# The bias of the output projection: from a matmul in each tile to a GpSimd addition on each tile of x

## The chip, the cores and the metric

The program runs on one core of one Trainium2 chip, in one launch. The metric is the device time of that core in microseconds (us), the median of several runs; less is better. The engines are named as the profile names them: PE (TensorE, with PEld for its weight loads), DVE (VectorE), ACT (ScalarE), POOL (GpSimd) and SP, whose queue issues most of the transfers.

## The reference, cut to what matters

```python
# x: [8, 1024, 512] float32; 16 heads of 32
qkv = x @ W_attn + b_attn
scores = k.q / sqrt(32), causal mask; attn = softmax over the keys
out = (attn @ v) reshaped to [8, 1024, 512]
x = layernorm(x + (out @ W_out + b_out))            # b_out: [512]
# then, per batch: the 1024 rows with the highest router score go through
# gelu(x @ W1 + b1) @ W2 + b2, are weighted, added back, and layernorm again
```

The change concerns `out @ W_out + b_out + x`. In the kernel the bias that is added is `b_out` plus the value part of `b_attn` times `W_out`, a single row of 512 numbers.

## The kernel before

**Units.** Attention is worked off in 64 units: a unit `u` is one batch, one group of four heads and one half `c = u % 2` of the queries (512). A half with c = 0 has 4 steps of 128 keys, one with c = 1 has 8 (`ksteps`). A step (u, k) is written here as (c, k).

**Slots and beats.** The program is laid out on a clock of slots of 16 beats, by the class `Table`. All five engine programs loop over the same beats `n`, and each engine does in beat `n` what the table puts there, in order; the engines meet only at semaphores. Two slots, an even and an odd one, are a period: they hold the scores of one odd and one even unit, and so on. The names in the code:

- `a_piece` (L1404) makes scores whose row maxima DVE takes (L1042, L1050); three PSUM banks in a ring. The maxima are turned (L1411), copied by DVE (L1061, L1063) and sent to `Qp` as a shift.
- `b_tile` (L1438) makes the scores again, transposed and shifted, in two PSUM banks in turn; ACT takes their exponential (L943) into one of `Pa`, `Pm` (two) and `P3` (in the trace `P`). A step's tiles must be read by ACT before PE can write the bank anew.
- POOL adds each step's probabilities onto `Pa`, head by head (L818), for the softmax sums, and clears the upper triangle of the diagonal steps with `keep` (L795). `pv` (L1456) on PE multiplies by V, and waits for `keep` where the step is on the diagonal. The buffer of step a is written again by ACT three steps later, once POOL has added it and PE has used it.
- `dense` on PE makes one piece (mostly one matmul) at a time of the projections in between: jobs K, Q (L1352), V (L1360), O (L1366, L1368), N (the softmax sums, L1375), with two PSUM banks taken in turn by the order of the jobs. A job waits for the evacuation of the job two before it.

**The output projection.** There are 64 jobs O, one for each tile of 128 rows. The first is in slot 10; up to batch 6 there is one in each slot, in beats 11 to 14, and those of batch 7 end in the slots after the last unit, between the first steps of the feed-forward part. Job `o` has its x tile in `xb[:, o % 2]`, loaded by SP (L708) some nine beats before the job starts, or, in the last batch, as late as one beat after it, since the slot must be stored first (L703, `ost`). PE does twelve matmuls of the split product and a thirteenth, `ones[0:97, :]` by `CB[0:97, :]` (L1368), which adds the bias: row 0 of `CB` is its high part and row 96 its rest. DVE then adds the PSUM tile onto `xb` (L1120), takes its statistics (L1122, L1253); POOL makes the scale and shift from them (L827, L828, L831, L834), and ACT writes the normalised tile to `hs` (L998) and to `xb` (L1000), which SP stores (L701, L703).

In POOL's program the additions of the steps formed in a beat stand first, then the four small instructions of the O job that ended in the beat before:

```python
for n in range(T.first, T.last):
    for u, k in T.steps_formed(n):
        ...
    for j in o_beat.get(n - 1, ()):
        ...
        e.wait_ge(s["lmva"], o + 1)
```

After the attention part comes the feed-forward part, from about 1880 us on; some of its steps are laid between the last O jobs.

Of the kernel before, what the change touches and what calls it, by code (L numbers as in the profile page):

```python
# [5 lines left out]
F32 = mybir.dt.float32  # L6
F32R = mybir.dt.float32r
# [6 lines left out]
P = 128  # L14
# [111 lines left out]
def dense_jobs(slot):  # L126
# [20 lines left out]
    if slot == 1:  # L147
        jobs.append(("C",))
    if 0 <= slot - 2 < U:
        jobs.append(("N", slot - 2))  # L150
# [4 lines left out]
PIECES = {"K": [1] * 12, "Q": [1] * 12, "V": [1] * 12, "O": [1] * 13, "T": [2], "S": [1], "N": [4], "C": [4] * 4}  # L155
TICKS = 54
# [18 lines left out]
class Table:  # L175
# [103 lines left out]
    def vector_in(self, n):  # L279

        now = self.ended.get(n, [])
        return [j for j in self.ended.get(n - 1, []) if j[0] in "KQT"] + [
            j for j in self.ended.get(n - 2, []) if j[0] == "N"] + [j for j in now if j[0] in "OCS"]
# [79 lines left out]
def layer(nc, s, args, dr, cs, out):  # L363
    T = Table()
    x, xt, wqkv, wo, bat, b_out, w_router, W1, b1, W2, b2 = args
    with ExitStack() as st:
# [63 lines left out]
        CB = sb("CB", [P, D], F32R)  # L430
# [13 lines left out]
        crow = hs[0:1, 0, :]  # L444
        ones = sb("ones", [P, P], F32R)
# [115 lines left out]
        o_beat, o_conv, o_load, t_load = T.o_beat, T.o_conv, T.o_load, T.t_load  # L561
        o_store = {}
# [186 lines left out]
        def gpsimd(e):  # L749
# [48 lines left out]
            for n in range(T.first, T.last):  # L798
                for u, k in T.steps_formed(n):
# [4 lines left out]
                    if a is not None and not by_products(u) and not in_sums(u, k):  # L804
# [9 lines left out]
                        for h0 in range(0, HG, many):  # L814
                            if h0 == (0 if k + 2 == ksteps(u) else 2) and kept_early(u, k + 1):
# [3 lines left out]
                                            ALU.add).then_inc(s["padd"], many)  # L819
                for j in o_beat.get(n - 1, ()):  # L820
# [205 lines left out]
        def vector(e):  # L1026
# [52 lines left out]
            def evacuate(job):  # L1079
# [27 lines left out]
                elif job[0] == "C":  # L1107
# [6 lines left out]
                    e.tensor_tensor(CB[96:97, :], crow, CB[0:1, :].bitcast(F32), ALU.subtract).then_inc(s["ev_v"], 1)  # L1114
                else:
# [3 lines left out]
                    e.wait_ge(s["xb", o % 2], 16 * (o // 2 + 1))  # L1119
# [177 lines left out]
        def tensor(e):  # L1297
            def wait_ready(job):
# [18 lines left out]
                elif kind == "T":  # L1317
                    e.wait_ge(s["hg", 0], 64)
                elif kind == "S":
                    e.wait_ge(s["score"], TT * (job[1] + 1))  # L1320
                else:
                    e.wait_ge(s["os"], o_number(job) + 1)
                    if o_number(job) == 0:
                        e.wait_ge(s["wo_lo"], 2)
                        e.wait_ge(*freed(("C",)))
# [11 lines left out]
            def dense(job, k):  # L1337
# [24 lines left out]
                elif kind == "O":  # L1362
                    if k < 12:
                        term, kt = divmod(k, KT)
                        oh, wh = ((0, 0), (1, 0), (0, 1))[term]
                        ins = e.matmul(to, Os[:, oh, kt, :], Wo[wh][:, kt, :], start=k == 0, stop=False)  # L1366
                    else:
                        ins = e.matmul(to, ones[0:97, :], CB[0:97, :], start=False, stop=True)  # L1368
# [13 lines left out]
                elif kind == "S":  # L1382
                    ins = e.transpose(to[0:TT, 0:P], sc[:, job[1], :], cs["identf"][:])
                else:
# [174 lines left out]
        with nc.Block() as block:  # L1559
# [8 lines left out]
              "wo_hi", "wo_lo", "x_hi", "x_lo", "ones", "rows", "d_mm", "ev_v", "ev_a", "kq_hi", "a_mm", "a_max",  # L1568
# [63 lines left out]
```

## Time and profile before

| | |
|---|---|
| median of 3 runs | 2560.07 us (2559.65 to 2562.88) |
| span of the profiled execution | 2558.8 us |
| PE busy | 2481.7 us (97%), 14168 matmuls |
| DVE, ACT, POOL busy | 1665.5 (65%), 1190.7 (47%), 1556.9 us (61%) |
| chain that ended last | PE 81%, POOL 2%, ACT 2%, DVE 1%, DMA 1% |
| mean granted TensorE clock | 0.981 |
| L1368, the thirteenth matmul | x64, 395 ns each in the trace |
| POOL busy, feed-forward part (1880 to 2558 us) | 154.76 of 678 us; PE 666.12 |

The profiled execution's span is 1.3 us under the median of the runs; that difference is the little that lies around the span. A matmul's time in the trace is that from its start to its last result; the next one starts before that, so what one costs PE is the distance between starts.

### The profile page before, as it was taken

What the parts mean: (1) busy time and instruction counts of PE and PEld (TensorE: products, weight loads), DVE (VectorE), ACT (ScalarE), POOL (GpSimd) and SP (SyncE); (2) the same over time, 40 slices, a digit from 0 to 9 for tenths busy, and PEclk for the clock granted to TensorE, in tenths of its full rate; (3) what the DMA queues carried; (4) which work ended last, traced back from release to release, by engine and by line L of the source; (5) the groups of instructions that cost most, each with busy time, mean ns of one, the idle gap of its engine ahead of it and who ended that gap; (6) DMA issues with size and microseconds to landing.
All of it is one profiled execution on the core that took longest, in us unless ns stands there. A gap on an engine that the chain in (4) does not pass through costs nothing.

```text
span 2558.8 us, 40698 instructions
## 1 busy us (share of the span) xinstructions
PE 2481.7 (97%) x14168; PEld 1834.9 (72%) x14168; DVE 1665.5 (65%) x4231; ACT 1190.7 (47%) x2034; POOL 1556.9 (61%) x1635
## 2 busy tenths in 40 slices
PE   7999999999999999999999999997999999999998
PEld 5666676777776777777776767773688888888886
DVE  6667677777776867877677777777555545553533
ACT  2555566656655655656656556565531111111110
POOL 1677788778887878888778877877232113121211
PEclk8999999999999999999999999998999999999999
DMA  7666677776577866767766676763420101010000
GB/s 146 90 108 139 126 144 172 140 150 157 129 144 130 193 128 127 175 127 153 151 145 146 125 167 137 155 154 97 152 91 25 34 25 42 25 34 25 22 29 17
DMA packets 167262, 286.46 MB, mean 112 GB/s; under 512 B 23121, under 2 KB 58001, under 8 KB 165906
## 3 DMA queue, kind: packets, MB, share of 16 engines
q1 hardware_dynamic: 159890, 267.01, 49.1%
q0 software_dynamic: 7168, 16.85, 2.1%
q8 instruction: 114, 1.87, 0.4%
q14 instruction: 90, 0.74, 0.1%
HBM read 116.97 MB, written 65.11 MB: 71 GB/s over the span
## 4 chain that ended last, share of the span: by engine, by line
PE 81%; POOL 2%; ACT 2%; DVE 1%; issue 1%; DMA 1%; SPq 1%; POOLq 0%; ACTq 0%; DVEq 0%
PE PS L1512 13%; PE PS L1491 13%; PE PS L1352 11%; PE PS L1438 10%; PE PS L1404 9%; PE PS L1456 8%; PE PS L1366 7%; PE PS L1360 6%; PE PS L1375 2%; POOL Pa L818 1%; PE PS L1368 1%; PE PS L1472 0%; PE PS L1333 0%; DMA h_s<-hs 0%; ACT Pm L943 0%
## 5 line engine op out<-in xcount | busy, mean ns | idle before, releaser
L818 POOL TENSOR_TENSOR Pa<-Pa,Pm 128x512 f32<-128x512 f32 (+1 forms) x602 | 743.8, 1259 | 114.4 <-ACT Pm L943 101.5
L1438 PE MATMUL PS<-Qp,Kp 98*128 98x512 f32 (+3 forms) x1536 | 494.9, 358 | 24.1 <-ACT Pm L943 13.2
L1404 PE MATMUL PS<-Kp,Qp 96*128 96x512 f32 (+3 forms) x1536 | 495.0, 359 | 17.4 <-DVE nm L1042 5.7
L943 ACT ACTIVATE Pm<-PS 128x512 f32<-128x512 f32 (+1 forms) x643 | 358.1, 568 | 282.6 <-PE PS L1438 243.5
L1042 DVE TENSOR_REDUCE nm<-PS 128x1 f32<-128x512 f32 x512 | 344.9, 687 | 183.7 <-PE PS L1404 183.6
L818 POOL TENSOR_TENSOR Pa<-Pa,P 128x512 f32<-128x512 f32 (+1 forms) x297 | 369.6, 1268 | 57.1 <-ACT P L943 50.1
L1404 PEld LDWEIGHTS PS<-Kp,Qp 96*128 96x128 f32 x1536 | 282.9, 193 | 118.5 <-issue 44.3
L1438 PEld LDWEIGHTS PS<-Qp,Kp 98*128 98x128 f32 x1536 | 281.7, 192 | 104.1 <-ACT Pm L943 27.4
L1050 DVE CUSTOM_DVE_ANT_0 PS<-PS,maskA 128x384 f32<-128x384 f32 (+3 forms) x512 | 245.9, 509 | 153.3 <-PE PS L1404 152.2
L908 ACT ACTIVATE G<-PS,b1c 128x512 f32<-128x512 f32 x128 | 88.2, 689 | 539.6 <-PE PS L1491 539.5
L1050 DVE CUSTOM_DVE_ANT_0 PS<-PS,maskA,nm 128x384 f32<-128x384 f32 (+3 forms) x512 | 267.0, 554 | 91.6 <-PE PS L1404 85.9
L1512 PE MATMUL PS<-W2h,Gs 128*128 128x512 f32 x1024 | 316.7, 390 | 0.9 <-DVE W2l L1144 0.9
L1491 PE MATMUL PS<-hT,W1h 128*128 128x512 f32 x1024 | 271.9, 389 | 0.0
L1195 DVE CAST Gs<-G 128x512 fp32r<-128x512 f32 x128 | 54.6, 427 | 306.9 <-ACT G L908 246.5
L943 ACT ACTIVATE P<-PS 128x512 f32<-128x512 f32 (+1 forms) x317 | 176.5, 569 | 132.8 <-PE PS L1438 115.1
L1491 PEld LDWEIGHTS PS<-hT,W1h 128*128 128x128 f32 x1024 | 192.1, 188 | 40.3 <-issue 0.2
L1512 PEld LDWEIGHTS PS<-W2h,Gs 128*128 128x128 f32 x1024 | 191.1, 188 | 40.0 <-issue 1.3
L943 ACT ACTIVATE Pa<-PS 128x512 f32<-128x512 f32 x256 | 149.1, 598 | 124.8 <-PE PS L1438 124.6
L1512 PE MATMUL PS<-W2l,Gs 128*128 128x512 f32 x512 | 199.2, 389 | 0.0
L783 POOL TENSOR_SCALAR rs<-mv 128x1 f32<-128x1 f32 x32 | 9.6, 301 | 304.8 <-DVE mv L1179 302.9
L1352 PE MATMUL PS<-xTh,Wkh 128*128 128x512 f32 x512 | 183.9, 412 | 8.8 <-ACT xTh L919 6.9
L1352 PE MATMUL PS<-xTh,Wkl 128*128 128x512 f32 x512 | 182.8, 411 | 0.0
(142 smaller groups left out, 4236.4 us busy)
## 6 DMA issues: line engine op xcount, KB each, us to landing
Qp<-nat SPq DMA_DIRECT2D x192, 256.0 KB, 7.4
Kp<-nat SPq DMA_DIRECT2D x192, 256.0 KB, 6.2
o_s<-Of SPq DMA_DIRECT2D x64, 256.0 KB, 2.3
Ot<-o_s SPq DMA_DIRECT2D x64, 256.0 KB, 3.1
xb<-in_x SPq DMA_DIRECT2D x64, 256.0 KB, 3.2
h_s<-hs SPq DMA_DIRECT2D x64, 256.0 KB, 2.3
out<-xb SPq DMA_DIRECT2D x64, 256.0 KB, 2.5
x_raw<-in_xt SPq DMA_DIRECT2D x15, 1024.0 KB, 6.4
```

The lines of the kernel that those rows point to most:

```text
L818: e.tensor_tensor(to, to, probs(u, k)[:, h0:h0 + many, 0:w], ALU.add).then_inc(s["padd"], many)
L943: e.activation(probs(u, k)[:, hh[0]:hh[-1] + 1, 0:w], tile_bank(j)[:, 0:len(hh) * w].rearrange("p (h n) -> p h n", n=w), ACT.Exp).then_inc ...
L1042: ins = e.tensor_reduce(out=nm[:, u % 2, 0, hh[0], qt:qt + 1], in_=PS[:, A_BANKS[j % 3], :], op=ALU.max, axis=AX, negate=True)
L1050: ins = e.tensor_tensor_reduce(out=to, in0=to, in1=maskA[:, 512 - w:512], scale=-1.0, scalar=least, op0=ALU.add, op1=ALU.min, accum_out=nm ...
L1352: ins = e.matmul(to, Wk[wh][:, 1 if kind == "K" else 0, kt, :], xT[xh][:, kt, c * 512:c * 512 + 512], start=k == 0, stop=k == 11)
L1360: ins = e.matmul(to[:, t * 256:t * 256 + 256], xT[xh][:, kt, tok:tok + P], Wv[wh][:, kt, :], start=m == 0, stop=m == 11)
L1366: ins = e.matmul(to, Os[:, oh, kt, :], Wo[wh][:, kt, :], start=k == 0, stop=False)
L1404: ins = e.matmul(to, Qp[0:96, u % 4, h_, qt * P:qt * P + P], Kp[0:96, (2 * i + k0 // 512) % 4, h_, 0:w], start=True, stop=True)
L1438: ins = e.matmul(tile_bank(j)[:, x_ * w:x_ * w + w], Kp[0:98, (2 * i + k // 4) % 4, h_, k % 4 * P:k % 4 * P + P], Qp[0:98, u % 4, h_, 512 ...
L1456: ins = e.matmul(PO[32 * h_:32 * h_ + 32, 512 - w:512], V[:, (u // 4 * 4 + k // 2) % 6, k % 2, vo:vo + HD], probs(u, k)[:, h_, 0:w], start ...
L1491: ins = e.matmul(PS[:, UP_BANKS[j % 2], :], W1p[wh][k][:, f * P:f * P + P], hT[:, xh, k, :], start=n_ == 0, stop=n_ == 11)
L1512: ins = e.matmul(PS[:, DOWN_BANK + t, :], Gs[:, j % 3, gh, t * P:t * P + P], W2p[wh][f // 4][:, f % 4, :], start=f == 0 and n_ == 0, stop= ...
```

## The change

The bias row is spread over the 128 partitions once, by one matmul of `ones` by `CB` (a new job R in slot 2) which DVE copies into the new tile `cB`. Job O has twelve matmuls, and the table has 53 ticks in a slot and not 54; no O job starts or ends in another beat, but 30 of the 64 Q jobs and 31 of the 64 V jobs end one beat later. At the beat in which an O job starts on PE, POOL adds `cB` to its x tile, behind the additions of that beat and ahead of the small instructions of the job before. DVE's addition of the PSUM tile waits for POOL's (`xc`) and no longer for the load of x. `CB` now lies in the space of `Os`.

```diff
@@ dense_jobs
+    if slot == 2:
+        jobs.append(("R",))
@@
-PIECES = {..., "O": [1] * 13, ...}
-TICKS = 54
+PIECES = {..., "O": [1] * 12, ..., "R": [4]}
+TICKS = 53
@@ layer
-        CB = sb("CB", [P, D], F32R)
+        cB = sb("cB", [P, D], F32)
+        CB = Os[:, 0, :, :].rearrange("p k n -> p (k n)")
+        biased = {}
+        for j in T.o_jobs:
+            biased.setdefault(T.start[j], []).append(j)
@@ gpsimd, in beat n, behind the additions of the steps
+                for j in biased.get(n, ()):
+                    o = o_number(j)
+                    if o == 0:
+                        e.wait_ge(*freed(("R",)))
+                    e.wait_ge(s["xb", o % 2], 16 * (o // 2 + 1))
+                    y = xb[:, o % 2, :]
+                    e.tensor_tensor(y, y, cB[:, :], ALU.add).then_inc(s["xc"], 1)
                 for j in o_beat.get(n - 1, ()):
@@ vector, evacuate
+                elif job[0] == "R":
+                    e.wait_ge(*done(job))
+                    e.tensor_copy(cB[:, :], src).then_inc(s["ev_v"], 1)
                 else:
                     o = o_number(job)
                     y = xb[:, o % 2, :]
                     e.wait_ge(*done(job))
-                    e.wait_ge(s["xb", o % 2], 16 * (o // 2 + 1))
+                    e.wait_ge(s["xc"], o + 1)
                     e.tensor_tensor(y, src, y, ALU.add).then_inc(s["ev_v"], 1)
@@ tensor, dense
-                    if k < 12:
-                        ...
-                    else:
-                        ins = e.matmul(to, ones[0:97, :], CB[0:97, :], start=False, stop=True)
+                    ... start=k == 0, stop=k == 11)
+                elif kind == "R":
+                    ins = e.matmul(to, ones[0:97, :], CB[0:97, :], start=True, stop=True)
```

Three places of POOL's queue. The first is the even slot with the O job number 26 (counted from 0), where the additions of an odd unit begin; L818 of before is L825 of the changed kernel, L795 is L802, and L827, L834 are L841, L848. Before:

```order
L818 TENSOR_TENSOR Pa<-Pa,P 128x512 [waits s_pv,s_padd,s_b_exp]
L818 TENSOR_TENSOR Pa<-Pa,P 128x512 x3
L818 TENSOR_TENSOR Pa<-Pa,Pm 128x512 [waits s_padd,s_b_exp]
L818 TENSOR_TENSOR Pa<-Pa,Pm 128x512 x3
L827 TENSOR_SCALAR lnrs<-lnmv 128x1 [waits s_oset,s_lmva]
```

In the changed kernel, at the same place:

```order
L825 TENSOR_TENSOR Pa<-Pa,P 128x512 [waits s_pv,s_padd,s_b_exp]
L825 TENSOR_TENSOR Pa<-Pa,P 128x512 x3
L833 TENSOR_TENSOR xb<-xb,cB 128x512 [waits s_xb_0]
L825 TENSOR_TENSOR Pa<-Pa,Pm 128x512 [waits s_padd,s_b_exp]
L825 TENSOR_TENSOR Pa<-Pa,Pm 128x512 x3
L841 TENSOR_SCALAR lnrs<-lnmv 128x1 [waits s_oset,s_lmva]
```

The addition of the bias stands between the four additions of step (1, 1) and those of step (1, 2), and ahead of everything that follows for the odd unit. The second is the odd slot behind it (job 27). Before:

```order
L795 AFFINE_SELECT P<-P 128x4x128 [waits s_b_exp,s_padd,s_keep]
L818 TENSOR_TENSOR Pa<-Pa,Pm 128x2x256 x2
L795 AFFINE_SELECT Pa<-Pa 128x4x128 [waits s_b_exp]
L827 TENSOR_SCALAR lnrs<-lnmv 128x1 [waits s_oset,s_lmva]
```

And in the changed kernel:

```order
L802 AFFINE_SELECT P<-P 128x4x128 [waits s_b_exp,s_padd,s_keep]
L825 TENSOR_TENSOR Pa<-Pa,Pm 128x2x256 x2
L833 TENSOR_TENSOR xb<-xb,cB 128x512 [waits s_xb_1]
L802 AFFINE_SELECT Pa<-Pa 128x4x128 [waits s_b_exp]
L841 TENSOR_SCALAR lnrs<-lnmv 128x1 [waits s_oset,s_lmva]
```

Here it stands behind the last `keep` (step (1, 7)) and the last additions of the odd unit, and ahead of the first `keep` of the next one. The third place is the last batch, where POOL has nothing else left. In the changed kernel (before, the same without L833):

```order
L833 TENSOR_TENSOR xb<-xb,cB 128x512 [waits s_xb_0]
L841 TENSOR_SCALAR lnrs<-lnmv 128x1 [waits s_oset,s_lmva]
L842 TENSOR_SCALAR lnrs<-lnmv 128x1
L845 TENSOR_TENSOR lnrs<-lnrs,half 128x2 [waits s_p_link]
L848 TENSOR_SCALAR lnnb<-lnrs,lnmv 128x2 [waits s_p_link]
```

There the addition for job `o`, which waits for the load of x tile `o`, stands ahead of the small instructions of job `o - 1`.

## Rows read from the trace of the kernel before

**Rows 1.** Windows: length, then each engine's busy us (instructions), PEclk, DMA share, GB/s.

```profile
1010.10:1042.00 31.90, 31.90 (x183) 22.04 (x181) 23.69 (x57) 18.23 (x33) 31.01 (x30) 1.00 0.58 103
1042.00:1063.60 21.60, 21.56 (x160) 16.25 (x160) 16.21 (x47) 15.44 (x28) 11.80 (x15) 1.00 0.87 217
```

**Rows 2.** Timeline of PE at the thirteenth matmul: start, length, engine, line, shapes, count.

```profile
1014.39 0.40 PE L1438 MATMUL PS<-Qp,Kp 98*128 98x512 f32 x1
1014.62 0.40 PE L1368 MATMUL PS<-CB,ones 97*128 97x512 f32 x1
1014.85 0.40 PE L1404 MATMUL PS<-Kp,Qp 96*128 96x512 f32 x1
```

**Rows 3.** Timeline of POOL over the additions of one odd unit (u = 35).

```profile
1010.11 5.03 POOL L818 TENSOR_TENSOR Pa<-Pa,P 128x512 f32<-128x512 f32 x4 [5.24 <-ACT P L943]
1015.28 5.00 POOL L818 TENSOR_TENSOR Pa<-Pa,Pm 128x512 f32<-128x512 f32 x4
...
1021.71 0.27 POOL L834 TENSOR_SCALAR lnnb<-lnrs,lnmv 128x2 f32<-128x2 f32 x1
1021.93 5.01 POOL L818 TENSOR_TENSOR Pa<-Pa,Pm 128x512 f32<-128x512 f32 x4
...
1038.83 0.64 POOL L795 TENSOR_SCALAR_AFFINE_SELECT P<-P 128x512 f32<-128x512 f32 x1
...
1042.59 0.64 POOL L795 TENSOR_SCALAR_AFFINE_SELECT Pa<-Pa 128x512 f32<-128x512 f32 x1 [0.64 <-ACT Pa L943]
```

**Rows 4.** Timeline of PE, the product of step (1, 7) of the same unit.

```profile
1039.61 0.43 PE L1456 MATMUL PS<-P,V 128*32 128x128 f32 x8
```

**Rows 5.** Timeline, the same keep and product of u = 11 and of u = 59.

```profile
387.93 0.63 POOL L795 TENSOR_SCALAR_AFFINE_SELECT P<-P 128x512 f32<-128x512 f32 x1
...
388.71 0.43 PE L1456 MATMUL PS<-P,V 128*32 128x128 f32 x8
...
1694.26 0.64 POOL L795 TENSOR_SCALAR_AFFINE_SELECT P<-P 128x512 f32<-128x512 f32 x1
...
1695.04 0.42 PE L1456 MATMUL PS<-P,V 128*32 128x128 f32 x8
```

**Rows 6.** Timeline of ACT and PE at the normalisation in the even slot.

```profile
1022.01 0.82 ACT L998 ACTIVATE hs<-xb,lnnb,lnrs 128x512 f32<-128x512 f32 x1 [0.28 <-POOL lnnb L834]
...
1023.43 1.06 ACT L943 ACTIVATE P<-PS 128x512 f32<-128x512 f32 x2
...
1024.06 0.50 PE L1438 MATMUL PS<-Qp,Kp 98*128 98x512 f32 x1
```

**Rows 7.** Timeline of DVE, the evacuation of O in both slots.

```profile
1015.19 0.68 DVE L1120 TENSOR_TENSOR xb<-PS,xb 128x512 f32<-128x512 f32 x1
...
1042.13 0.69 DVE L1120 TENSOR_TENSOR xb<-PS,xb 128x512 f32<-128x512 f32 x1 [0.58 <-PE PS L1368]
```

**Rows 8.** Timeline and windows at two stalls of PE at batch ends.

```profile
863.28 0.50 PE L1438 MATMUL PS<-Qp,Kp 98*128 98x512 f32 x1 [1.78 <-ACT P L943]
...
864.40:867.80 3.40, 3.40 (x20) 3.01 (x19) 3.40 (x9) 1.85 (x4) 3.32 (x4) 1.00 0.07 26
...
1079.41 0.50 PE L1438 MATMUL PS<-Qp,Kp 98*128 98x512 f32 x1 [1.78 <-ACT Pm L943]
...
1080.50:1083.90 3.40, 3.40 (x12) 3.01 (x11) 3.40 (x9) 0.97 (x3) 3.32 (x4) 0.50 0.05 17
```

**Rows 9.** Timeline of POOL in the last batch, jobs 60 and 61.

```profile
1852.18 0.28 POOL L827 TENSOR_SCALAR lnrs<-lnmv 128x1 f32<-128x1 f32 x1 [5.12 <-DVE lnmv L1253]
...
1854.08 0.27 POOL L834 TENSOR_SCALAR lnnb<-lnrs,lnmv 128x2 f32<-128x2 f32 x1
...
1860.59 0.28 POOL L827 TENSOR_SCALAR lnrs<-lnmv 128x1 f32<-128x1 f32 x1 [6.25 <-DVE lnmv L1253]
```

**Rows 10.** DMA issues of the page: KB each, median us from issue to landing.

```profile
xb<-in_x SPq DMA_DIRECT2D x64, 256.0 KB, 3.2
...
out<-xb SPq DMA_DIRECT2D x64, 256.0 KB, 2.5
```

More of the change, by code:

```diff
@@ L151, in dense_jobs @@
     return jobs
-PIECES = {"K": [1] * 12, "Q": [1] * 12, "V": [1] * 12, "O": [1] * 13, "T": [2], "S": [1], "N": [4], "C": [4] * 4}
-TICKS = 54
+PIECES = {"K": [1] * 12, "Q": [1] * 12, "V": [1] * 12, "O": [1] * 12, "T": [2], "S": [1], "N": [4], "C": [4] * 4,
+          "R": [4]}
+TICKS = 53
 FIRST_SLOT, LAST_SLOT = -2, U + 5
@@ L282, in vector_in @@
         return [j for j in self.ended.get(n - 1, []) if j[0] in "KQT"] + [
-            j for j in self.ended.get(n - 2, []) if j[0] == "N"] + [j for j in now if j[0] in "OCS"]
+            j for j in self.ended.get(n - 2, []) if j[0] == "N"] + [j for j in now if j[0] in "OCSR"]
     def x_half(self, job):
@@ L1318, in wait_ready @@
                     e.wait_ge(s["hg", 0], 64)
+                elif kind == "R":
+                    e.wait_ge(*freed(("C",)))
                 elif kind == "S":
@@ L1324, in wait_ready @@
                         e.wait_ge(s["wo_lo"], 2)
-                        e.wait_ge(*freed(("C",)))
                 if d >= 2:
@@ L1362, in dense @@
                 elif kind == "O":
-                    if k < 12:
-                        term, kt = divmod(k, KT)
-                        oh, wh = ((0, 0), (1, 0), (0, 1))[term]
-                        ins = e.matmul(to, Os[:, oh, kt, :], Wo[wh][:, kt, :], start=k == 0, stop=False)
-                    else:
-                        ins = e.matmul(to, ones[0:97, :], CB[0:97, :], start=False, stop=True)
+                    term, kt = divmod(k, KT)
+                    oh, wh = ((0, 0), (1, 0), (0, 1))[term]
+                    ins = e.matmul(to, Os[:, oh, kt, :], Wo[wh][:, kt, :], start=k == 0, stop=k == 11)
                 elif kind == "N":
@@ L1383, in dense @@
                     ins = e.transpose(to[0:TT, 0:P], sc[:, job[1], :], cs["identf"][:])
+                elif kind == "R":
+                    ins = e.matmul(to, ones[0:97, :], CB[0:97, :], start=True, stop=True)
                 else:
@@ L1567 @@
 SEMAPHORES = ("c0", "bias", "b_scaled", "wq_in", "w1_in", "x0_hi", "rk0", "w_in", "w_hi", "w_split", "w_st", "v_in", "v_hi", "v_split", "v_st", "wo_in",
-              "wo_hi", "wo_lo", "x_hi", "x_lo", "ones", "rows", "d_mm", "ev_v", "ev_a", "kq_hi", "a_mm", "a_max",
+              "wo_hi", "wo_lo", "x_hi", "x_lo", "ones", "rows", "xc", "d_mm", "ev_v", "ev_a", "kq_hi", "a_mm", "a_max",
               "shift", "b_mm", "b_exp", "keep", "padd", "pv", "o_cp", "nln", "rinv", "ot", "os_hi", "os",
```

## The prediction, on record before the changed kernel ran

> **What bounds the kernel now.** I read the page first: PE is busy 97% of the span and makes 81% of the chain that ended last, POOL is busy 61%. Taken as averages these say that a matmul saved is time saved, and that POOL has room. The question is what holds within one period of two slots, so I then read the windows view over one of them. It falls into two parts [rows 1]: from 1010.1 to 1042.0 us POOL is busy 31.01 of 31.90 us, and from 1042.0 to 1063.6 only 11.80 of 21.60. POOL's 61% hides a stretch of 32 us in which it never rests.
>
> The timeline of POOL shows what that stretch is [rows 3]. It starts when ACT has formed step (1, 1) (POOL had idled 5.24 us and waited for `P`), and from there POOL works off the additions and keeps of the odd unit without a gap worth the name until 1042 us, several us behind ACT. The end that counts is the keep of step (1, 7), 1038.83 + 0.64 = 1039.47 us. PE's product for that step starts at 1039.61 [rows 4], 0.14 us behind it. That is no accident of one period: I paired keep and product in all 26 odd units from 9 to 59 whose burst will hold a bias addition. In 22 of them the distance is 0.14 or 0.15 us (first and last shown here: 387.93 + 0.63 to 388.71, and 1694.26 + 0.64 to 1695.04 [rows 5]); in the other four, at batch ends, it is 1.0 to 1.2. A distance that never varies is that of a released wait. So PE has about nothing in hand here, and the loop of a period is: PE and ACT form step (1, 1); POOL's burst, 29.4 us to the keep; PE goes on for 24 us to the next step (1, 1).
>
> The same stretch has a second place where POOL is what is waited for [rows 6]. In the even slot POOL's small instructions for the O job end at 1021.71 + 0.27 = 1021.98; ACT's L998 starts at 1022.01, after an idle 0.28 us that it spent on them. Behind it in ACT's queue are L1000 and then two exponentials at 1023.43, and PE's next score tile at 1024.06 follows the first of them (half of 1.06 us, so 1023.96) by 0.1 us or less: with two banks it needs that one emptied.
>
> **The change, part by part.**
>
> *Removed: 64 matmuls.* The start before, the thirteenth and the start after are 0.23 us apart each [rows 2]: (1014.85 - 1014.39) / 2 = 0.23. At most 64 x 0.23 = 14.9 us, where PE sets the pace. The 0.40 us of a row is not the price, since starts overlap.
>
> *Added: 64 POOL additions of 128x512.* The same operation on the same shape is L818: four in 5.00 us [rows 3], 1.25 us each. The DVE addition that they precede takes 0.69 [rows 7]. The Trainium skill, GPSIMD Engine Reference, section Engine selection, says that elementwise work on a tile belongs on VectorE, GpSimd being about two times slower for two inputs. By that rule the trace agrees (1.25 against 0.69, 1.8 times); by it alone the addition is badly placed, but it puts no time on the whole.
>
> *Where they stand.* The order of POOL's queue puts the even slot's addition between the steps (1, 1) and (1, 2), that is inside the burst, at 1015.2 us. The x tile has long landed then. Nothing in the burst is idle that could take it, so all behind it is 1.25 us later: the small instructions, L998 and L1000 on ACT, the two exponentials, and so PE's tile at 1024.06; and the keep of (1, 7). These are one delay seen at two places, not two: once PE is held 1.25 us at 1024, it meets the keep in the same step as now. Price: +1.25 us per period, 26 periods, +32.5 us. The even slot's saved 0.23 us does not count, PE only arrives earlier at the wait.
>
> *The odd slot's addition* stands behind the burst's last additions and ahead of the keep that came at 1042.59 [rows 3]. POOL has room from there on [rows 1], so it does not lengthen the loop. But DVE's L1120 wanted to start at 1042.13 and now waits for it: about 1.25 us, as in the even slot (POOL at 1015.14, L1120 at 1015.19 [rows 3, 7]). Behind it on DVE stand L1122, the copies of the shift, L1253, and the maxima of the next scores. I followed the first of these to PE: the A ring needs the maxima from three entries back, and DVE had idled between 1.3 and 1.8 us before the first maxima of each slot, which takes most of a delay of 1.25. The PSUM bank is needed by the job two later, over 1.5 us away. So I cost DVE's wait at nothing; if that cover were gone it would be up to 1.25 us for each of 52 slots. The saved 0.23 us of the odd slot does count, as it lies in the part that PE paces: 26 x -0.23 = -6.0, unless the next unit's first product, whose keep is now also later, takes it back: 0 to 6.0. I take half. Steady part: 32.5 - 3.0 = 29.5, between 26.5 and 32.5.
>
> *The last batch.* For ten O jobs after that (54 to 63) the matmul saves 10 x 0.23 = 2.3 us. Against it stands a new loop in POOL's queue. The addition for job o waits for the load of x tile o, which waits for the store of tile o - 2, and it stands ahead of the small instructions of job o - 1, on which the store of tile o - 1 hangs. Once that is tight, a tile takes: addition 1.25, small instructions 1854.35 - 1852.18 = 2.2 [rows 9], ACT's two passes 1.6 [rows 6], store 2.5, load 3.2 [rows 10], in all 10.75, about 11 with the handovers. Now a tile takes 1860.59 - 1852.18 = 8.4 us [rows 9]. It becomes tight at about job 60, so the last evacuation is some 3 x 2.6 = 8 to 9 us late. PE there reads what DVE and ACT make two feed-forward steps later, so much of this is hidden; from nothing to 9 us reaches PE, and I take 4. Net +2 (-2 to +7). From 1880 us on PE is busy 666 of 678 us and everything shifts by what has gathered.
>
> *The rest.* Job R is one matmul and one DVE copy in slot 2; Q and V jobs that end a beat later are read many beats on. Nothing, at worst 1 us.
>
> Sum, against the profiled execution's own 2558.8 us: +29.5 +2 = 2590.3. The median of the runs stands 1.3 us above the span, so 2591.6 us.
>
> **The rivals.**
>
> *The clock falls too.* Twice PE stood for 1.78 us at the end of a batch [rows 8]. After the one at 1079.41 the granted clock was 0.50 for the next 3.4 us, the lower of its two levels, and PE started 12 matmuls there; after the one at 863.28 it stayed at 1.00, with 20. My new stall at 1024 is 1.25 us, with the 0.23 that PE arrives earlier about 1.5, a little shorter. If each brings a stretch at 0.50, half of 3.4 us is lost, 1.7 us, 26 times: +44, 2636 us; if half of them do, about 2614. The Trainium skill, TensorE: Matmul & The Clock Gate, section Part 1, says that the chip gates this clock by how busy PE has been; the trace agrees in the one case and not in the other. Since stalls shorter than 1.78 us leave no such mark that I found, I give it 0.18 in all.
>
> *POOL has room after all, and the saving is kept.* If PE's 0.14 us behind the keep is PE's own pace, and the normalisation has slack in ACT, the additions fall into POOL's idle 9.8 us of the second part and 64 x 0.23 remains: 2560.1 - 14.9 = 2545. It decides whether POOL's burst can be 1.25 us longer without PE seeing it. Against it: the constancy over 22 units, and ACT's wait. 0.08.
>
> *It is a draw.* The delay is partly taken up (half of 1.25 us) and the savings cover the rest: 2555 to 2565. 0.03. Between this and the forecast, 2565 to 2583, with only some of the periods held: 0.07.
>
> *DVE's waits reach PE.* If L1120's delay stalls the A ring by another 0.5 us in each slot, 52 x 0.5 = 26 on top, 2618. It is in the same direction as the clock; I count it with 0.04.
>
> **How the numbers follow.** The forecast, the burst longer by one addition, has 0.60: 2591.5, its own range 2583 to 2604. The range 2574 to 2620 adds the greater part of the held-in-some-periods case, DVE's and the milder half of the clock's; it leaves out the rest of the clock's (0.08), the fast case (0.08) and the draw (0.03). What a measurement of this kernel can tell from no change is about 0.2%, 5 us. Faster 0.08, same 0.03, slower 0.89.
>
> **What would show it.** POOL's burst from the first addition of (1, 1) to the keep of (1, 7) grows from 29.4 to about 30.6 us, with L833 in it at 1.25. ACT's wait for `lnnb` in the even slot grows from 0.28 to about 1.5 us, and PE waits over 1 us for an exponential right behind it. DVE's L1120 (new number) waits 1.2 us for `xb` of POOL in nearly every slot. In the last batch the distance of tiles grows from 8.4 to about 11 us. It is wrong if the burst is longer but the product follows it at more than 0.14 us; if PE waits at neither place; or if the stretches at clock 0.50 are many more than now.

## The result and the profile after

The changed kernel takes 2607.9 us (median of 4 runs, 2602.8 to 2610.2) against 2560.0 for the kernel before (4 runs): 1.0173 times, 95% interval 1.016 to 1.0187. It is slower, by 48 us; the prediction was 2591.5, in a range of 2574 to 2620. Direction and mechanism were right. The size was 16 us short: 2607.9 lies above the forecast's own range of 2583 to 2604, and within the wider one only because that had been stretched for two rivals.

The page of the changed kernel, its span and the busy time of each engine, and below two groups of its part 5:

```profile
span 2606.8 us, 40638 instructions
PE 2485.0 (95%) x14105; PEld 1827.5 (70%) x14105; DVE 1669.2 (64%) x4232; ACT 1185.6 (45%) x2034; POOL 1636.2 (63%) x1699
L1455 PE MATMUL PS<-Qp,Kp 98*128 98x512 f32 (+3 forms) x1536 | 499.5, 362 | 54.7 <-ACT Pm L957 33.1
L1421 PE MATMUL PS<-Kp,Qp 96*128 96x512 f32 (+3 forms) x1536 | 500.5, 362 | 20.3 <-DVE nm L1064 10.1
```

Groups of instructions by line and form, of the changed kernel (busy us, mean ns of one, idle us before and what ended it):

```profile
L833 POOL TENSOR_TENSOR xb<-xb,cB 128x512 f32<-128x512 f32 x64 | 82.3, 1286 | 35.1 <-DMA xb<-in_x 35.0
L1012 ACT ACTIVATE hs<-xb,lnnb,lnrs 128x512 f32<-128x512 f32 x64 | 52.0, 812 | 89.8 <-POOL lnnb L848 89.8
L1137 DVE TENSOR_TENSOR xb<-PS,xb 128x512 f32<-128x512 f32 x64 | 44.2, 691 | 90.2 <-POOL xb L833 81.2 <-PE PS L1383 8.9
L1275 DVE CUSTOM_DVE_ANT_0 hs<-hs,wrB 128x512 f32<-128x512 f32 x64 | 69.2, 1081 | 31.0 <-DMA h_s<-hs 30.8
```

The averages say little once more: POOL went from 61% to 63%. The groups say where to look. The 64 additions cost 82.3 us on POOL (1.29 each); ACT waited 89.8 us for POOL's small LayerNorm results, 44.6 before; DVE waited 81.2 us for the biased x tile; PE stood 54.7 us before its score tiles, 24.1 before the change. And DVE waited 30.8 us for the store of h (17.1 before), which the prediction had not looked at.

Timelines of POOL, ACT, PE and DVE of the changed kernel in the period that [rows 3, 4, 6, 7] show for the kernel before:

```profile
1029.96 5.02 POOL L825 TENSOR_TENSOR Pa<-Pa,P 128x512 f32<-128x512 f32 x4 [5.03 <-ACT P L957]
1034.94 1.28 POOL L833 TENSOR_TENSOR xb<-xb,cB 128x512 f32<-128x512 f32 x1
1036.18 5.00 POOL L825 TENSOR_TENSOR Pa<-Pa,Pm 128x512 f32<-128x512 f32 x4
...
1042.62 0.27 POOL L848 TENSOR_SCALAR lnnb<-lnrs,lnmv 128x2 f32<-128x2 f32 x1
...
1059.84 0.64 POOL L802 TENSOR_SCALAR_AFFINE_SELECT P<-P 128x512 f32<-128x512 f32 x1
...
1042.92 0.82 ACT L1012 ACTIVATE hs<-xb,lnnb,lnrs 128x512 f32<-128x512 f32 x1 [1.33 <-POOL lnnb L848]
...
1044.97 0.50 PE L1455 MATMUL PS<-Qp,Kp 98*128 98x512 f32 x1 [0.98 <-ACT P L957]
...
1060.62 0.42 PE L1473 MATMUL PS<-P,V 128*32 128x128 f32 x8 [0.22 <-POOL P L802]
...
1064.31 0.69 DVE L1137 TENSOR_TENSOR xb<-PS,xb 128x512 f32<-128x512 f32 x1 [1.74 <-POOL xb L833]
```

The addition sits in the burst behind step (1, 1). From 1029.96 the burst lasts to 1060.48, 30.5 us instead of 29.4, and PE's product still follows the keep at 0.14 us. ACT waits 1.33 us for `lnnb` where it waited 0.28 [rows 6], and PE's tile behind it waits 0.98 us for the exponential. The marks that the prediction named for this stretch are there, if not in their exact sizes: it had "over 1 us" for PE's wait, and 1.2 us for DVE's wait for `xb`, which is 1.74 here.

So far this period, u = 35, runs like any ordinary one. But it is the first of a pair at the end of a batch, and there it gets worse: ACT and DVE also split the next batch's x. Timelines of the changed kernel at the end of the same period and in the next one, and the window that follows:

```profile
1079.49 0.69 DVE L1275 CUSTOM_DVE_ANT_0 hs<-hs,wrB 128x512 f32<-128x512 f32 x1 [4.52 <-DMA h_s<-hs]
...
1081.01 0.47 PE L1421 MATMUL PS<-Kp,Qp 96*128 96x512 f32 x1 [1.35 <-DVE nm L1064]
...
1098.23 0.66 POOL L841 TENSOR_SCALAR lnrs<-lnmv 128x1 f32<-128x1 f32 x1
...
1099.23 1.38 POOL L845 TENSOR_TENSOR lnrs<-lnrs,half 128x2 f32<-128x2 f32 x1
...
1101.02 0.81 ACT L1012 ACTIVATE hs<-xb,lnnb,lnrs 128x512 f32<-128x512 f32 x1 [2.87 <-POOL lnnb L848]
...
1104.02 0.79 PE L1455 MATMUL PS<-Qp,Kp 98*128 98x512 f32 x1 [3.72 <-ACT Pm L957]
...
1104.60:1108.00 3.40, 3.40 (x11) 2.80 (x10) 2.49 (x4) 1.41 (x3) 3.32 (x4) 0.50 0.00 0
```

Two stalls of PE, one in each period of the pair. The second one was there before, 1.78 us [rows 8]; now it is 3.72 us, and behind it the clock column reads 0.50, the lower of TensorE's two levels.

I cut periods from one start of (1, 1) on POOL to the next, and take 26, from u = 9 to u = 61 (303.3 to 1760.7 us in the changed kernel, 304.7 to 1719.0 before). Twelve of them are the six pairs at batch ends (u = 11 and 13, 19 and 21, and so on), 14 are ordinary:

| us of the profiled execution | before | changed | difference |
|---|---|---|---|
| 14 ordinary periods | 750.7 | 764.0 | +13.3 |
| 12 batch-end periods | 663.6 | 693.4 | +29.8 |
| start of period 61 to the end | 839.8 | 846.1 | +6.3 |
| up to period 9 | 304.7 | 303.3 | -1.4 |

The parts come from one execution of each kernel, and differences of a few us between them mean little: e4 and e8 below run the same program over these 26 periods and need 1416.3 and 1419.5 us, the changed kernel and e5 likewise 1457.4 and 1461.2.

An ordinary period costs +0.95 us: the burst +1.15 and the way back from keep to (1, 1) -0.20, the odd slot's matmul. At that pace 26 periods would be +24.7, and the prediction had 26.5 to 32.5 for them. The rest stands in the twelve periods.

### The profile page after: what moved, and what is told of

Its sections match the earlier page's. It is cut to its first block and busy times, and to the rows that moved or that the text cites. A ratio compares the mean times of both kernels' runs of the same rounds, so it can differ in the third digit from the quotient of the medians.

```text
span 2606.8 us, 40638 instructions
## 1 busy us (share of the span) xinstructions
PE 2485.0 (95%) x14105; PEld 1827.5 (70%) x14105; DVE 1669.2 (64%) x4232; ACT 1185.6 (45%) x2034; POOL 1636.2 (63%) x1699
## 5 line engine op out<-in xcount | busy, mean ns | idle before, releaser
L825 POOL TENSOR_TENSOR Pa<-Pa,Pm 128x512 f32<-128x512 f32 (+1 forms) x602 | 741.0, 1256 | 111.7 <-ACT Pm L957 101.4
L1455 PE MATMUL PS<-Qp,Kp 98*128 98x512 f32 (+3 forms) x1536 | 499.5, 362 | 54.7 <-ACT Pm L957 33.1
L1421 PE MATMUL PS<-Kp,Qp 96*128 96x512 f32 (+3 forms) x1536 | 500.5, 362 | 20.3 <-DVE nm L1064 10.1
L825 POOL TENSOR_TENSOR Pa<-Pa,P 128x512 f32<-128x512 f32 (+1 forms) x297 | 367.4, 1262 | 55.1 <-ACT P L957 49.7
L1064 DVE CUSTOM_DVE_ANT_0 PS<-PS,maskA,nm 128x384 f32<-128x384 f32 (+3 forms) x512 | 260.8, 551 | 94.8 <-PE PS L1421 94.1
L1383 PE MATMUL PS<-Woh,Os 128*128 128x512 f32 x512 | 176.6, 408 | 9.4 <-DVE Os L1263 9.4
```

Of the source, the lines that this page charges most:

```text
L825: e.tensor_tensor(to, to, probs(u, k)[:, h0:h0 + many, 0:w], ALU.add).then_inc(s["padd"], many)
L1064: ins = e.tensor_tensor_reduce(out=to, in0=to, in1=maskA[:, 512 - w:512], scale=-1.0, scalar=least, op0=ALU.add, op1=ALU.min, accum_out=nm ...
L1421: ins = e.matmul(to, Qp[0:96, u % 4, h_, qt * P:qt * P + P], Kp[0:96, (2 * i + k0 // 512) % 4, h_, 0:w], start=True, stop=True)
L1455: ins = e.matmul(tile_bank(j)[:, x_ * w:x_ * w + w], Kp[0:98, (2 * i + k // 4) % 4, h_, k % 4 * P:k % 4 * P + P], Qp[0:98, u % 4, h_, 512 ...
```

## The experiments

In the tables below "steady" is the span from period 9 to 61, "rest" from there to the end. Each ratio is to runs of the kernel before that were made alongside; they had 2560.65 us for e1 to e4, 2563.1 for e5 to e7, 2563.0 for e8 and e9, 2560.2 for e10 and e11.

### e1 to e4: which of the two additions, and where

e1 is the kernel before with twelve matmuls and 53 ticks in a slot; its output lacks the bias of the output projection.

```diff
-                    if k < 12:
-                        ...
-                    else:
-                        ins = e.matmul(to, ones[0:97, :], CB[0:97, :], start=False, stop=True)
+                    term, kt = divmod(k, KT)
+                    ...
+                    ins = e.matmul(to, Os[:, oh, kt, :], Wo[wh][:, kt, :], start=k == 0, stop=k == 11)
```

> The kernel before without the thirteenth matmul and without any other addition of the bias: the bias of the output projection is left out. What the removed matmuls are worth by themselves. Burst theory (GpSimd's chain sets PE's pace at step (1, 7)): only the odd slot's matmul and the ten of the last batch count, 36 x 0.23 = 8.3 us, so about 2552 us, and the product of (1, 7) still starts 0.14 us behind its keep. Rival (PE sets its own pace all through): 64 x 0.23 = 14.9 us, 2545 us, and the distance grows to about 0.4 us.

e2 and e3 add to e1 one POOL addition at each even (e2) or odd (e3) O job of the first 54, that is 27 additions, on a tile that nobody reads; the bias is missing as well.

```diff
+                if n in extra:
+                    ...
+                    e.tensor_tensor(y, y, wrB[:, :], ALU.add)
```

> e1 plus one GpSimd addition of 128x512 into a tile that nobody reads, in the even slots only (27 of them), where the changed kernel has its bias addition: its bias is left out. DVE waits for nothing new. Burst theory: each period is 1.25 us longer, the four or six at batch ends by more, so 32 to 42 us over e1, 2584 to 2594 us. Rival (GpSimd has room, and it is DVE's new wait that costs in the changed kernel): within 3 us of e1.

> The same with the addition in the odd slots only, behind the last additions of the odd unit. The bias is left out. Burst theory: GpSimd has room there, so within 4 us of e1. Rival (each addition costs the same wherever it stands): as e2, some 32 us over e1.

e4 is the changed kernel with all its work, the even slots' additions one beat earlier, ahead of the burst.

```diff
-            biased.setdefault(T.start[j], []).append(j)
+            o = o_number(j)
+            biased.setdefault(T.start[j] - (o % 2 == 0 and o < 54), []).append(j)
```

> The changed kernel with the even slots' bias addition one beat earlier, where GpSimd idles before the burst; the odd slots and the last batch as they are. All work is done. Burst theory: the 26 x 1.25 us and the extra at batch ends that comes from them are gone; what is left over the kernel before is what the odd slots' wait of DVE costs at batch ends and the last batch, so 2560 to 2575 us. Rival (DVE's waits in the odd slots carry half of the loss): 2580 us or more.

| kernel | time, us | ratio to before (95%) | ordinary | batch ends | steady | rest |
|---|---|---|---|---|---|---|
| e1, no bias | 2547.2 | 0.995 (0.9933 to 0.9966) | 749.4 | 655.7 | 1405.2 | 835.5 |
| e2, even | 2585.4 | 1.0091 (1.0073 to 1.0108) | 763.9 | 682.1 | 1446.0 | 837.3 |
| e3, odd | 2547.5 | 0.9951 (0.9934 to 0.9967) | 749.9 | 657.5 | 1407.4 | 833.4 |
| e4, even one beat early | 2566.1 | 1.0024 (1.0013 to 1.0034) | 749.6 | 666.7 | 1416.3 | 843.2 |

The matmul is worth 13.4 us of the 14.9 that its spacing allowed, though hardly any in the ordinary periods (-1.3 us in 14). There PE only arrives earlier at the keep. Timelines of POOL and PE of e1:

```profile
1033.73 0.63 POOL L795 TENSOR_SCALAR_AFFINE_SELECT P<-P 128x512 f32<-128x512 f32 x1
...
1034.52 0.43 PE L1453 MATMUL PS<-P,V 128*32 128x128 f32 x8 [0.20 <-POOL P L795]
```

It is earned at batch ends (-7.9), at the start and in the last batch (-4.3). Of the -7.9 some 3.6 are one period, u = 51 (57.0 us before, 53.4 in e1), in which the profiled execution of the kernel before had a stall of PE of 2.0 us with a low clock behind it, and e1's had none. So e1's time, taken alone, lay nearer the rival's 2545 than the forecast's 2552, and only the timeline told them apart.

e2 against e1 is the price of an addition inside the burst with nobody waiting for it: +38 us. e3 is the same work 16 beats later: 0.3 us more than e1. e4 moves the even addition by one beat out of the burst and gives back 42 us. All three came within the range that the burst theory gave them. Each is all or nothing, so POOL's load is not what costs; the place is.

But e4 keeps 11 us over e1 in the steady part and 8 in the rest. e3 has the odd slot's POOL work too, without the wait of DVE for it, and has neither. The next runs look there.

### e5 to e7: the last batch, the odd slot, and a second addition

e5 is the changed kernel with the addition behind the small instructions of the same beat, which changes the order in the last batch alone (one later load on SP waits for the last addition as well).

```diff
-                for j in biased.get(n, ()):
-                    ...
                 for j in o_beat.get(n - 1, ()):
                     ...
+                for j in biased.get(n, ()):
+                    ...
```

> The changed kernel, with GpSimd's bias addition placed behind its small LayerNorm instructions of the same beat instead of ahead of them. In the first 52 O slots the two stand in different beats, so only the last batch's order changes there. The changed kernel took 2607.9 us; from period 61 to the end its profile has 846.1 us, the kernel before 839.8, the changed kernel without the bias 835.5. Theory A (in the last batch the additions stand ahead of the small instructions on which the LayerNorm waits, and this reaches TensorE): the stretch from period 61 falls by 4 to 6 us, the time to 2602 to 2604. Theory B (the 6.3 us of the last batch come from elsewhere, late transfers or the clock): the stretch stays within 1.5 us of 846.1 and the time within 2 us of 2608.

e6 has the order of e5, and both additions of a period one beat ahead of the even slot.

```diff
-            load = self.start[j] - 9
+            load = self.start[j] - (25 if o % 2 and o < 54 else 9)
...
-            biased.setdefault(T.start[j], []).append(j)
+            o = o_number(j)
+            biased.setdefault(T.start[T.o_jobs[o - o % 2]] - 1 if o < 54 else T.start[j], []).append(j)
```

> The changed kernel with all its work, but the bias additions of the even and of the following odd O slot both stand one beat ahead of the even slot, in front of GpSimd's burst (the odd slot's x tile is loaded 25 beats ahead instead of 9), and in the last batch behind the small LayerNorm instructions. The early even addition alone gave 2566.1 us, with 11.2 us over the kernel without bias in periods 9 to 61 and 7.7 us in the rest. Theory A (those 11.2 us are the odd slot's LayerNorm waiting for its late addition, so that the stores of h land late at a batch's end, and the 7.7 us are the order in the last batch): both vanish, periods 9 to 61 come to 1405 to 1410 us, the time to 2548 to 2556, below both the kernel before (2560.6) and the changed one. Theory B (the 2.5 us of two additions in front of the burst are more than the room there, or the earlier load delays other transfers at a batch's end): some of it comes back in every period, periods 9 to 61 stay at 1416 us or over, and the time at 2562 or over.

e7 is e2 with a second addition behind the first (the same line twice, the second waiting for the first).

> The kernel before without thirteenth matmul and without bias, with two GpSimd additions of 128x512 to a tile that nobody reads in each of the first 26 even O slots, inside the burst (one such addition gave 2585.4 us, none 2547.2; the second waits for the first). The output lacks the bias. Theory A (GpSimd's burst sets the end of each period, so that each further addition costs its whole length of about 1.25 us in each of 26 periods, plus the excess at batch ends): another 33 to 40 us, 2619 to 2625. Theory B (the first addition cost mostly because it pushed the kernel into another regime, a low clock or late transfers, and the second one lies beside that): less than 20 us more, under 2605.

| kernel | time, us | ratio to before (95%) | ordinary | batch ends | steady | rest |
|---|---|---|---|---|---|---|
| e5, order of the last batch | 2601.3 | 1.0144 (1.0127 to 1.0161) | 763.9 | 697.4 | 1461.2 | 839.0 |
| e6, both early | 2562.4 | 0.9997 (0.9987 to 1.0006) | 757.6 | 663.0 | 1420.6 | 836.6 |
| e7, two in the burst | 2637.6 | 1.0288 (1.0271 to 1.0305) | 794.6 | 701.6 | 1496.2 | 835.4 |

**e5** gives back 7.1 us in the rest (6.6 us of the whole time), a little more than the 4 to 6 expected and all of the +6.3: the loop of the last batch was the whole of that term. In the changed kernel POOL's queue stands for the load of x with the small instructions of the job before behind it, 9.5 to 10.3 us a tile, and PE pays. Timeline of POOL and PE in the last batch of the changed kernel:

```profile
1883.73 1.39 POOL L833 TENSOR_TENSOR xb<-xb,cB 128x512 f32<-128x512 f32 x1 [6.53 <-DMA xb<-in_x]
1885.21 0.19 POOL L841 TENSOR_SCALAR lnrs<-lnmv 128x1 f32<-128x1 f32 x1
...
1894.03 1.29 POOL L833 TENSOR_TENSOR xb<-xb,cB 128x512 f32<-128x512 f32 x1 [6.66 <-DMA xb<-in_x]
...
1890.23 0.50 PE L1383 MATMUL PS<-Woh,Os 128*128 128x512 f32 x1 [1.00 <-DVE Os L1263]
```

The view of waits, of the changed kernel and then of e5 (us in total, times, longest), PE for the projection's input:

```profile
PE PS L1383 <- DVE Os L1263: 9.4, 5, 4.5
```

```profile
PE PS L1384 <- DVE Os L1264: 4.5, 1, 4.5
```

**e6** cured the last batch too and missed 2548 to 2556: theory B's number. Its trace shows why. Timelines of POOL before two bursts, and of PE in the second:

```profile
406.60 1.73 POOL L851 TENSOR_TENSOR xb<-xb,cB 128x512 f32<-128x512 f32 x1
411.12 1.29 POOL L851 TENSOR_TENSOR xb<-xb,cB 128x512 f32<-128x512 f32 x1 [2.80 <-DMA xb<-in_x]
...
519.39 0.60 POOL L856 TENSOR_SCALAR sg<-sg 128x8 f32<-128x8 f32 x1 [1.63 <-ACT sg L1021]
520.07 1.66 POOL L858 TENSOR_TENSOR sg<-sg,minus 128x8 f32<-128x8 f32 x1
521.70 2.55 POOL L851 TENSOR_TENSOR xb<-xb,cB 128x512 f32<-128x512 f32 x2
...
538.15 0.50 PE L1457 MATMUL PS<-Qp,Kp 98*128 98x512 f32 x1 [1.24 <-ACT P L959]
```

The room before the burst holds two additions, but once a batch the gate's two small instructions (2.3 us) stand there as well, and once a batch the x tile comes late. The gate's instructions push the burst back and cost 1.3 us in each of six periods (54.8 us instead of 53.5). At the batch ends there is in turn no stall of PE for K or for maxima left; two for ACT have grown to 3.19 us from start to start (2.18 before).

**e7** missed both theories, upwards: the second addition cost some 50 us (50.2 in the steady part), more than the first with 38. In POOL's queue it takes 1.46 us a period with the handovers, 38 us in all, which is theory A. The rest is the clock. PE's wait in the even slot is now some 2.46 us, and behind the one at 608.45 the clock is 0.50, behind the one at 1069.09 it is not. Timeline of PE and the windows behind these two stalls, of e7:

```profile
608.45 0.50 PE L1448 MATMUL PS<-Qp,Kp 98*128 98x512 f32 x1 [2.47 <-ACT Pm L956]
1069.09 0.50 PE L1448 MATMUL PS<-Qp,Kp 98*128 98x512 f32 x1 [2.46 <-ACT P L956]
...
610.10:613.50 3.40, 3.40 (x12) 2.93 (x11) 2.84 (x11) 0.97 (x2) 3.32 (x4) 0.50 0.38 80
1069.60:1073.00 3.40, 3.40 (x20) 2.97 (x20) 2.68 (x11) 2.28 (x5) 3.32 (x4) 1.00 0.16 63
```

PE started 12 matmuls in one and 20 in the other. The steady part of e7 has 78 us at 0.50, e2's has 31; half of the difference, 24 us, is the most that it can have cost. What it did cost can be read from e7's ordinary periods with u of 15 and over: the seven with one such stretch took 57.0 to 57.1 us, the six without 55.9 to 56.1. So a stretch of 3.4 us costs about 1.05 us here, and the difference of 48 us some 15. With the 38 us of POOL's queue that covers the 50.

### e8 and e9: putting it together

e8 is e4 with the order of e5. e9 is e6 with the odd addition early only in every second period, which leaves out the two collisions:

```diff
-            load = self.start[j] - (25 if o % 2 and o < 54 else 9)
+            load = self.start[j] - (25 if o % 4 == 3 and o < 54 else 9)
...
-            biased.setdefault(T.start[T.o_jobs[o - o % 2]] - 1 if o < 54 else T.start[j], []).append(j)
+            early = o < 54 and (o % 2 == 0 or o // 2 % 2)
+            biased.setdefault(T.start[T.o_jobs[o - o % 2]] - 1 if early else T.start[j], []).append(j)
```

> The changed kernel with all its work, the even slots' bias additions one beat earlier (alone 2566.1 us) and the last batch's additions behind the small LayerNorm instructions (alone 6.6 us gained); the odd slots' additions of the first 26 periods stay where the change has them. Theory A (the two costs are independent and in different stretches): periods 9 to 61 as with the early even addition alone, 1416 us, the rest 836 to 839 as with the tail order alone, time 2559 to 2561, equal to the kernel before. Theory B (the tail's gain needs the late state that the changed kernel arrives in): 2564 to 2567.

> As e6_both_early, but the odd slot's addition is moved in front of the burst only in every second period (those in which, in e6's trace, it neither waited 2.8 us for its x tile nor met the 2.3 us of the gate's small instructions that GpSimd has once a batch); in the others it stays at its own slot. Theory A (GpSimd has room for two additions in front of the burst except in those periods, and the early odd addition cures the two-microsecond stall of the first period of each batch's end that the early even addition left): the 1.3 us that e6 lost in each of six periods vanish, periods 9 to 61 come to 1410 to 1414 us, the time to 2553 to 2556, below the kernel before by 0.2 to 0.3%. Theory B (what costs in e6 is the earlier load of x and its collisions, whichever period it stands in): 2560 or over.

| kernel | time, us | ratio to before (95%) | ordinary | batch ends | steady | rest |
|---|---|---|---|---|---|---|
| e8 | 2560.6 | 0.9993 (0.9984 to 1.0002) | 749.7 | 669.8 | 1419.5 | 837.5 |
| e9 | 2552.5 | 0.9958 (0.9945 to 0.9971) | 749.9 | 660.6 | 1410.5 | 836.3 |

e8 hit theory A; e9 did too, 0.5 us under its range. e9 does all the work and beats the kernel before by 0.4% and the changed one by 2.1%, keeping some 10 of the 13.4 us that the matmul is worth. Timelines of POOL and ACT of e9, the same places as above:

```profile
1003.57 1.28 POOL L852 TENSOR_TENSOR xb<-xb,cB 128x512 f32<-128x512 f32 x1
1006.35 1.30 POOL L852 TENSOR_TENSOR xb<-xb,cB 128x512 f32<-128x512 f32 x1 [1.50 <-DMA xb<-in_x]
1008.66 5.02 POOL L828 TENSOR_TENSOR Pa<-Pa,P 128x512 f32<-128x512 f32 x4 [1.01 <-ACT P L960]
1013.82 5.00 POOL L828 TENSOR_TENSOR Pa<-Pa,Pm 128x512 f32<-128x512 f32 x4
...
1020.54 0.81 ACT L1015 ACTIVATE hs<-xb,lnnb,lnrs 128x512 f32<-128x512 f32 x1 [0.26 <-POOL lnnb L844]
```

Both additions lie in what was POOL's idle time before (1, 1), 1.01 us of it is left, and ACT waits 0.26 us for `lnnb` as it did before the change.

### e10 and e11: is it the store of h?

What is left in e8 is a stall of PE of some 2 us in the first period of four of six batch ends. Just before it DVE stands for a store of h. These two kernels let DVE take the gate's score, which waits for that store, three beats later in seven of eight tiles.

```diff
-                for j in o_beat.get(n - 7, ()):
+                for j in scores.get(n, ()):
```

> As e8_even_tail (odd additions in their own slots, 2560.6 us, periods 9 to 61 1419.5 us), with VectorE's gate score, which waits for the store of h, three beats later for the first seven tiles of each batch but the last. In e8's trace VectorE stood 4.3 us for that store at 1059.67 us, and TensorE stood 2.16 us at 1061.91, a stall of this kind in four of six batch ends. Theory A (the score's wait for the late store blocks VectorE's queue, maxima and the tiles behind them come late, and that is the odd addition's price): no stall of 2 us is left in the first period of a batch end, its excess falls by 6 to 12 us, the time to 2549 to 2554. Theory B (the transfers of the K pieces are late for another reason, the stretch of large loads at a batch's end): the stalls stay, the time is within 3 us of 2560.6.

> As e9_mixed_early (2552.5 us, periods 9 to 61 1410.5 us, one such stall at a batch's end, 2.15 us), with the same later score. Theory A: the one stall goes, 1.5 to 4 us, 2548 to 2551. Theory B: within 2 us of 2552.5.

| kernel | time, us | ratio to before (95%) | ordinary | batch ends | steady | rest |
|---|---|---|---|---|---|---|
| e10 (e8, later score) | 2560.1 | 0.9998 (0.9988 to 1.0007) | 755.6 | 663.1 | 1418.7 | 834.4 |
| e11 (e9, later score) | 2559.6 | 0.9995 (0.9985 to 1.0004) | 756.3 | 662.9 | 1419.3 | 836.3 |

The stall of e8 in PE's timeline, then DVE's wait for the store and PE's wait for one group of the maxima in the view of waits, first of e8 and then of e10:

```profile
1061.91 0.47 PE L1423 MATMUL PS<-Kp,Qp 96*128 96x512 f32 x1 [1.87 <-DMA Kp<-nat]
...
DVE hs L1277 <- DMA h_s<-hs: 29.6, 7, 4.7
...
PE PS L1423 <- DVE nm L1066: 5.2, 6, 1.8
```

```profile
PE PS L1427 <- DVE nm L1070: 18.2, 30, 1.0
...
DVE hs L1281 <- DMA h_s<-hs: 4.8, 1, 4.8
```

The trace follows theory A: none of the four stalls is left, and the batch ends are 6.7 us shorter. The time does not: each ordinary period is 0.4 us longer, 5.9 us in 14, and the gain is gone; e11 even lost its lead, outside what either theory gave it. The traces show where it goes. Timelines of DVE and PE of e10 in an ordinary period (u = 23):

```profile
711.32 1.50 DVE L1281 CUSTOM_DVE_ANT_0 hs<-hs,wrB 128x512 f32<-128x512 f32 x1
713.29 0.14 DVE L1070 DVE_READ_ACCUMULATOR2_ANT nm<- 128x1 f32 x1
...
713.48 0.50 PE L1427 MATMUL PS<-Kp,Qp 96*128 96x512 f32 x1 [0.68 <-DVE nm L1070]
```

Three beats later the score stands in DVE's queue right ahead of maxima that PE waits for. PE waits for that group of maxima 30 times, 18.2 us in all, where in e8 it did 6 times, 5.2 us. The difference is 13.0 us; 26 periods that are 0.43 us longer make 11.2.

The stalls themselves follow DVE's wait for the store closely. In the first periods of the six pairs, over the eleven traces in which the score has its old place, DVE's wait was 4.08 to 5.15 us in 19 cases, and in all 19 PE stalled there for K or maxima, over 1.2 us from start to start. In the other 47 cases the wait was 0.86 to 3.87 us, and PE did not stall so once. One of the 19 is in the kernel before, u = 51, with a wait of 4.88 us and a stall of 2.00, so it takes no addition to come so far. The mean wait over the six periods is 2.4 us before, 1.5 in e1, 1.9 in e3, 4.3 in the changed kernel, 3.7 and 4.2 in e4 and e8, 2.8 in e9; the even addition has a part in it too (3.4 in e2), though not in e7 (1.7), and why that is so no run shows. So the long wait for the store is shown as the cause of those stalls, and moving the score by three beats is no cure.

## Why the prediction was right, and where it was short

**The burst** (+1.25 us a period, even slot): right. e2 against e1 shows it alone, e4 undoes it by one beat. It measured +1.15, and the way back from the keep -0.20. The rule of the Trainium skill that the prediction cited (GPSIMD Engine Reference, Engine selection) bears on the length of the addition only, 1.29 us here against the 0.69 of a DVE addition of the same shape, and e9 shows that a slower engine with room at the right beat is still the cheaper one. The saving of the odd slot was kept almost whole in ordinary periods (0.20 of 0.23 us), where the prediction took half. As a steady pace, +24.7 us instead of the +29.5 in the sum.

**All 26 periods cost the same** was the step that failed. The prediction knew the stalls at batch ends [rows 8], used them for a rival, and counted these twelve periods like the rest in the sum. They cost +29.8 us, at the ordinary pace 11.4, so 18 us more. Read from the changed kernel's trace, from start to start on PE: the six stalls for ACT grew from 2.18 to 4.13 us, not by 1.15 but by 1.95 (+4.8 over the burst's share); stalls in the first period of a pair came in four of six ends (1.29, 1.64, 1.92 and 2.21 us, each 0.23 being pace), where the kernel before had one of 2.00 (+4.4); and 37.5 us at the low clock instead of 17.1, which is at most +10.2, and some 6 at e7's price. Together 19.4 with the clock at its most, 15 to 16 at e7's price; the 18 lie between them, and the spread of these parts between executions is 3 to 4 us.

*The growth to 4.13.* In e2, where nobody waits for the addition, these stalls are 3.55 to 3.59. The other 0.55 go with POOL's small instructions L841 and L845, which take 0.66 and 1.38 us there (0.52 and 0.71 in e2) while DVE works at the split of x (L1156, two inputs from SBUF). The Trainium skill, GPSIMD Engine Reference, section Key points, says that GpSimd shares its SBUF interfaces with VectorE and contends with its instructions of two SBUF inputs. Timelines of POOL and DVE of e2, then DVE's split in the changed kernel beside its L845 at 1099.23:

```profile
1095.57 0.71 POOL L838 TENSOR_TENSOR lnrs<-lnrs,half 128x2 f32<-128x2 f32 x1
1095.70 0.68 DVE L1146 TENSOR_TENSOR xTl<-x_raw,xTh 128x512 fp32r<-128x512 f32 x1
```

```profile
1099.37 0.67 DVE L1156 TENSOR_TENSOR xTl<-x_raw,xTh 128x512 fp32r<-128x512 f32 x1
```

The stretched rows fit that section. One row of e2 does not: its L838 ran beside the same split and took 0.71 us, as the same instruction does in ordinary periods. So the overlap alone does not explain the 1.38 us, and what stretches L845 stays open.

*The stalls in the first periods.* There are four in the changed kernel, five in e5, two in e4 and four in e8, all with the odd addition in its slot; none in e1 and in e3, which does the same work on POOL without DVE's wait, none in e6 and one in e9 with it moved. It is not the odd addition alone: e2 without it has two short ones (1.24 and 1.56 us), the kernel before has one, and e4 and e8, alike in this stretch, have two and four. With the odd slot's LayerNorm late, DVE waits longer for the store of h, and a wait of over 4 us there is what reaches PE.

**DVE's wait for the odd slot, costed at nothing**: right in ordinary periods (e3 and e8 stand at 749.9 and 749.7 us), wrong at batch ends. I followed the maxima behind L1137 and stopped there; the store of h, which DVE itself waits for later in its queue, was not on my list. With the odd addition moved where that is safe, e9's steady part is 9 us below e8's, so that is about its price, give or take the 3 to 4 us by which such parts differ between executions.

**The last batch** (+4 less 2.3): the loop was named and its cause right; the distance of tiles went from 8.4 to between 9.5 and 10.3 us, less than the 11 I had, but over the last six tiles instead of four. It measured +6.3, inside -2 to +7; the order alone is worth 7.1 (e5).

**The clock rival** came true in part, and not where I put it. The new stall, 1.38 us from start to start in 13 ordinary periods and in the first of each pair, was followed by no low stretch at all. The eight low stretches (five before) all go with batch-end stalls. So the prediction's own sign of being wrong, many more stretches at 0.50, is met in part, and at the batch ends alone: eight for five, 37.5 us for 17.1. It is no case apart, then, but an addition to the forecast's mechanism, and a low stretch costs about 1.05 us (e7) and not the 1.7 that the rival took. The Trainium skill, TensorE: Matmul & The Clock Gate, section Part 1, has the clock follow how busy PE has been; the traces of the last section agree at both ends, in that stalls for ACT up to 1.9 us kept it and those from 3.5 us on lost it; two of 3.19 us in e6 kept it all the same.

**POOL has room after all** was half right in a way that I had not written down: POOL has the room, 5 us before the burst, one beat from where the addition was put. With it there, e9 is faster than the kernel before.

**That the measured time lies in the range** is in part luck. The range went up to 2620 for a clock that falls behind the new stall in half of the periods, and for DVE's wait stalling PE in every slot; neither happened in that form. What filled it were the batch ends.

## What to carry to other kernels

Whether an engine has room is a question of the beat, not of its share: with the same 64 additions the kernel was 48 us slower or 10 us faster than before, by whether they stood in the stretch that the loop waits for or just ahead of it. Multiply a per-period cost only by the periods that look alike; those that already show a stall get their own term, as a stall that grows there brings late stores and a lower clock with it. When an instruction gets later, follow everything its engine will wait for later on, transfers too, and not only the next consumer.

## What the runs showed that I had not expected

- The cost of a delay was not proportional: the first addition in the burst cost 38 us, the second some 50.
- One beat (53.5 us by 32, so 1.7 us) decided about 42 us in e4.
- The granted clock behind stalls of PE for ACT in the even slot, by their length from start to start, in periods 9 to 59 of all thirteen traces: up to 1.41 us never at 0.50 in 66 cases; 1.63 to 1.93 us never in 10; 2.15 to 2.20 us at 0.50 in 29 of 49; 2.87 us (e7) in 10 of 19; 3.19 us (e6) in none of 2, 3.29 us in 1 of 1; 3.55 us and over (the changed kernel, e2, e5, e7, six each) in 24 of 24. A low stretch lasted 3.4 or 6.8 us there. What decides in the cases between, these rows do not show. The window behind one of the stalls of 3.19 us, at 867.79 us of e6, with the clock at 1.00:

```profile
868.30:871.70 3.40, 3.40 (x20) 2.97 (x20) 3.38 (x7) 2.29 (x5) 3.32 (x4) 1.00 0.00 1
```
